# Causal masks added by TensorE in the bank of the row maxima, one plain maximum a head

## What is computed

```
# first block: 8 heads of 16, 4 key heads, window of 128 and 4 sink columns
allowed = (j <= i) & ((j < SINKS) | (j >= i - WINDOW + 1))
scores = jnp.where(allowed, q @ k.T * SCALE + directions, -jnp.inf)
# second block: 16 heads of 8, 4 key heads
scores = jnp.where(jnp.tril(ones(256, 256)), q @ k.T / np.sqrt(8), finfo.min)
# third block (second layer): 16 heads of 8, no mask
attn = jax.nn.softmax(scores, axis=-1); out = attn @ v
```

## Time and profile before

| | |
|---|---|
| three runs | 2305.39, 2350.81, 2354.41 us |
| median | 2350.81 us |
| span of the profiled execution | 2378.5 us |
| mean granted TensorE clock in it | 0.850 of full speed |
| PE, DVE, ACT, POOL busy | 91%, 48%, 38%, 17% |
| first pass | about 60 to 472 us |
| second pass | about 500 to 1240 us |
| expert network | about 1240 to 1560 us |
| third pass | about 1580 to 2180 us |

### The profile page before, as it was taken

One profiled execution on the slowest core, in us unless ns is written; L12 is line 12 of the kernel. 1 busy time (PEld: TensorE's weight loads), 2 busy tenths in 40 slices (PEclk: granted clock), 3 DMA queues, 4 the chain that ended last, 5 costly groups with the idle time before them and its releaser, 6 DMA issues.

```text
span 2378.5 us, 35332 instructions
## 1 busy us (share of the span) xinstructions
PE 2162.3 (91%) x11152; PEld 1350.9 (57%) x11152; DVE 1141.0 (48%) x4250; ACT 894.1 (38%) x1820; POOL 404.1 (17%) x643
## 2 busy tenths in 40 slices
PE   5999999879999999999989999969999999999490
PEld 3666666545555555555557888844555555554260
DVE  3344545354444444443428888845554545444102
ACT  1243434423343344343452222214554444554130
POOL 2111211121111121121100000022121212121505
PEclk8598989957686788786889999958998999999595
DMA  6000000000000000000000000010000000000132
GB/s 211 1 1 1 0 1 0 1 0 1 1 1 2 1 1 2 1 1 1 1 1 1 1 0 0 1 36 1 1 1 2 1 2 1 1 1 2 48 107 75
DMA packets 26218, 30.38 MB, mean 13 GB/s; under 512 B 3744, under 2 KB 19392, under 8 KB 25664
## 3 DMA queue, kind: packets, MB, share of 16 engines
q1 hardware_dynamic: 24000, 24.08, 3.2%
q0 software_dynamic: 2048, 4.20, 0.6%
HBM read 19.88 MB, written 8.39 MB: 12 GB/s over the span
## 4 chain that ended last, share of the span: by engine, by line
PE 86%; DVE 4%; issue 3%; POOL 2%; ACT 2%; another core or an unknown queue 1%; DMA 1%; SPq 0%; POOLq 0%; DVEq 0%; ACTq 0%
PE ps_out L1812 25%; PE ps_four L1794 8%; PE ps_four L997 5%; PE ps_max L1008 5%; PE ps_max L1764 4%; PE ps_max L1759 3%; PE ps_four L1718 3%; PE ps_four L1674 3%; PE ps_work L1699 3%; PE ps_max L1760 2%; PE ps_four L1699 2%; PE ps_work L1679 2%; PE ps_four L1787 2%; PE ps_four L1796 2%; PE ps_work L1658 2%
## 5 line engine op out<-in xcount | busy, mean ns | idle before, releaser
L1812 PE MATMUL ps_out<-attn_f,v_all 128*9 128x256 f32 (+3 forms) x2560 | 654.7, 384 | 5.8 <-ACT attn_f L1383 5.2
L1394 ACT ACTIVATE attn_f<-ps_four 128x384 f32<-128x384 f32 (+1 forms) x640 | 340.5, 532 | 627.2 <-PE ps_four L1796 618.4
L1812 PEld LDWEIGHTS ps_out<-attn_f,v_all 128*9 128x9 f32 (+1 forms) x2560 | 196.1, 96 | 273.9 <-issue 78.1
L1794 PE MATMUL ps_four<-q_st,k_st 26*128 26x256 f32 (+1 forms) x640 | 263.3, 411 | 0.2 <-DVE q_st L1602 0.2
L1581 DVE CUSTOM_DVE_ANT_0 ps_max<-ps_max,q_masks 128x128 f32<-128x128 f32 (+1 forms) x768 | 256.2, 377 | 0.0
L1588 DVE TENSOR_REDUCE row_max<-ps_max 128x2 f32<-128x512 f32 x256 | 170.1, 686 | 132.7 <-PE ps_max L1764 132.6
L1383 ACT COPY attn_f<-ps_out 9x512 f32<-9x512 f32 (+1 forms) x320 | 183.8, 575 | 132.1 <-PE ps_out L1812 132.1
L1794 PEld LDWEIGHTS ps_four<-q_st,k_st 26*128 26x128 f32 (+1 forms) x640 | 127.8, 200 | 75.6 <-issue 26.2
L1796 PE MATMUL ps_four<-q_st,k_st 26*128 26x256 f32 (+2 forms) x640 | 164.8, 258 | 0.0
L1574 DVE COPY wait_cell<-one 128x1 f32<-128x1 f32 x384 | 56.9, 148 | 186.3 <-PE ps_max L1760 181.2
L1008 PEld LDWEIGHTS ps_max<-wd,o_both 128*128 128x128 f32 x1024 | 134.7, 193 | 18.7 <-DVE o_both L904 8.3
(11 more groups left out here) (250 smaller groups left out, 3423.0 us busy)
## 6 DMA issues: line engine op xcount, KB each, us to landing
wd<-in_L_ffn_W SPq DMA_DIRECT2D x16, 256.0 KB, 2.6
gates_all<-in_select SPq DMA_DIRECT2D x3, 1024.0 KB, 7.3
x_all<-in_L_attn_x SPq DMA_DIRECT2D x8, 256.0 KB, 6.0
slots_dram<-attn_f SPq DMA_DIRECT2D x8, 256.0 KB, 5.5
h_tok<-slots_dram SPq DMA_DIRECT2D x8, 256.0 KB, 2.7
y_dram<-o_both SPq DMA_DIRECT2D x8, 256.0 KB, 2.4
out_x<-x_all SPq DMA_DIRECT2D x16, 128.0 KB
wgu<-in_L_ffn_Wg SPq DMA_DIRECT2D x1, 1024.0 KB, 5.8
```

What stands on the lines that cost most here:

```text
L1394: nc.scalar.activation(probs[:, h % 4, 0:w], ps_exp[:, h % 3, 0:w], ACT.Exp, scale=c.scale).then_inc(exp_done, 1)
L1794: nc.tensor.matmul(bank[:, 0:S], k_st[rows, r, g, 0:P], q_st[rows, r, g, :], start=not c.causal, stop=True, skip_group_check=True)
L1812: last = nc.tensor.matmul(ps_out[0:c.hd + 1, (h % 2) * S + first:(h % 2 + 1) * S], v_tok[c.index][:, r, kb, kv, :], probs[:, h % 4, kb * S ...
```

## The change

The row maxima get their masks as the exponentials do. TensorE first writes 384 columns of masks into the bank (ident_bf times three blocks), and the two score matmuls add onto them. VectorE takes one tensor_reduce over three blocks of 128 columns instead of two masked reductions, and no small copies. The second and the third block both belong to queries 128 to 255, so once a batch, after the last head, one small tensor_tensor takes the maximum of the two for all heads; the step "rows" waits for it by a new semaphore. The array masks now holds three blocks for each of the two orientations. exp_scores writes its masks by one matmul of 384 columns in both causal passes; in the second pass the middle block is zero, which VectorE sets at the start of that pass, and TensorE waits for that once.

```diff
-        masks = sb("masks", [P, 2, P], BF16)
+        masks = sb("masks", [P, 2, 3, P], BF16)
...
-        row_max = sb("row_max", [P, 2, BLK, 16])
-        wait_cell = sb("wait_cell", [P, 6])
-        q_masks = sb("q_masks", [P, 3, P])
+        row_max = sb("row_max", [P, 2, 3, 16])
...
-            nc.vector.tensor_copy(q_masks[:, 0, :], squares[:, 1, :])
-            nc.vector.tensor_copy(q_masks[:, 1, :], squares[:, 2, :])
-            nc.vector.tensor_copy(q_masks[:, 2, :], squares[:, 1, :]).then_inc(pro_dve, 1)
-            dve.wait_ge(pro_dve, 9)
...
-            nc.gpsimd.tensor_copy(masks[:], squares[:, 3:5, :])
+            for side, square in enumerate((1, 3)):
+                nc.gpsimd.tensor_copy(masks[:, side, 0:2, :], squares[:, square:square + 2, :])
+                nc.gpsimd.tensor_copy(masks[:, side, 2, :], squares[:, square, :])
...
                 dve.wait_ge(max_mm, hn + 1)
-                if c.causal:
-                    nc.vector.tensor_copy(wait_cell[:, h % 4:h % 4 + 1], one[:])
                 if h == 0:
                     at_least(dve, mt_mm, n - 1)
-                    if c.causal and not isinstance(n, int):
-                        nc.vector.tensor_copy(wait_cell[:, 4 + r2:5 + r2], one[:])
-                if c.causal:
-                    for k, (first, last) in enumerate(((0, P), (P, 3 * P))):
-                        ins = nc.vector.tensor_tensor_reduce(
-                            ps_max[:, h % 2, first:last], ps_max[:, h % 2, first:last],
-                            q_masks[:].rearrange("p n m -> p (n m)")[:, first:last], 1.0, LEAST, ALU.add, ALU.max,
-                            row_max[:, r2, k, h:h + 1])
-                    ins.then_inc(max_done, 1)
-                else:
-                    src = ps_max[:, h % 2, 0:c.q_cols()].rearrange("p (k s) -> p k s", k=BLK)
-                    nc.vector.tensor_reduce(row_max[:, r2, :, h], src, AX_X, ALU.max).then_inc(max_done, 1)
+                blocks = 3 if c.causal else 2
+                src = ps_max[:, h % 2, 0:c.q_cols()].rearrange("p (k s) -> p k s", k=blocks)
+                nc.vector.tensor_reduce(row_max[:, r2, 0:blocks, h], src, AX_X, ALU.max).then_inc(max_done, 1)
+                if c.causal and h == c.heads - 1:
+                    dve.wait_ge(max_done, hn + 1)
+                    nc.vector.tensor_tensor(row_max[:, r2, 1, 0:c.heads], row_max[:, r2, 1, 0:c.heads],
+                                            row_max[:, r2, 2, 0:c.heads], ALU.max).then_inc(row_max_done, 1)
...
-                    nc.vector.memset(q_masks[:, 1, :], 0.0).then_inc(window_open, 1)
-                    dve.wait_ge(window_open, 1)
+                    nc.vector.memset(masks[:, :, 1, :], 0.0).then_inc(window_open, 1)
...
                 if c.causal:
-                    nc.tensor.matmul(bank[:, 0:P], q_st[rows, r, g, 0:P], k_st[rows, r, g, 0:P], start=True, stop=True)
-                    nc.tensor.matmul(bank[:, P:3 * P], q_st[rows, r, g, P:S], k_st[rows, r, g, :], start=True,
-                                     stop=True).then_inc(max_mm, 1)
+                    nc.tensor.matmul(bank[:, 0:3 * P], ident_bf[:], masks[:, 0].rearrange("p n m -> p (n m)"),
+                                     start=True, stop=False, skip_group_check=True)
+                    nc.tensor.matmul(bank[:, 0:P], q_st[rows, r, g, 0:P], k_st[rows, r, g, 0:P], start=False,
+                                     stop=True, skip_group_check=True)
+                    nc.tensor.matmul(bank[:, P:3 * P], q_st[rows, r, g, P:S], k_st[rows, r, g, :], start=False,
+                                     stop=True, skip_group_check=True).then_inc(max_mm, 1)
...
                 if c.causal:
-                    nc.tensor.matmul(bank[:, 0:P], ident_bf[:], masks[:, 0, :], start=True, stop=False,
-                                     skip_group_check=True)
-                    nc.tensor.matmul(bank[:, S:S + P], ident_bf[:], masks[:, 0, :], start=False, stop=False,
-                                     skip_group_check=True)
-                    if c.window:
-                        nc.tensor.matmul(bank[:, P:S], ident_bf[:], masks[:, 1, :], start=False, stop=False,
-                                         skip_group_check=True)
+                    nc.tensor.matmul(bank[:, 0:3 * P], ident_bf[:], masks[:, 1].rearrange("p n m -> p (n m)"),
+                                     start=True, stop=False, skip_group_check=True)
...
-                    pe.wait_ge(max_done, HEADS_BEFORE[c.index] + (b + 1) * c.heads)
+                    if c.causal:
+                        pe.wait_ge(row_max_done, n + 1)
+                    else:
+                        pe.wait_ge(max_done, HEADS_BEFORE[c.index] + (b + 1) * c.heads)
...
+                if c.index > 0:
+                    pe.wait_ge(window_open, 1)
```

More of the change, by code:

```diff
@@ L22 @@
 LN_EPS = 1e-5
-LEAST = -3e38
 MASKED = -1e30
@@ L335, in adaln_two_layers @@
         max_done = sem("max_done")
+        row_max_done = sem("row_max_done")
         mt_mm = sem("mt_mm")
@@ L975, in pe_prologue @@
             last.then_inc(pro_pe, 1)
-            pe.wait_ge(pro_dve, 10)
+            pe.wait_ge(pro_dve, 9)
             pe.wait_ge(ones_ready, 2)
```

## The result

The changed kernel takes 2462.9 us (median of 4 runs, 2455.9 to 2483.7) against 2337.0 us of the kernel before (4 runs beside it, 2305.4 to 2354.4): 126 us more. The ratio that goes with the comparison, which leaves out runs over 1.5% above the fastest of their kernel, is 1.064 [1.054, 1.074]: slower.

The account below looks back on a forecast made before the run. The prediction took TensorE's instruction sequence to bound both causal passes. 40.4 us (first pass) plus 115.3 (second) plus 4 (openings) less 10 gave +150 us, 6.3%, or 2499 us on 2350.8; range 2430 to 2590 us.

Parts of the forecast that it names:

- Mask to strip: Causal heads' maxima: from the new 384-column mask matmul to the first score matmul, 0.26 us at the high clock.
- second head: Second head of a pair in the maxima, free before, now costs 0.68 us at the high level, 1.18 at the low.
- The credit for the step to a strip: Leading heads' masks: 0.09 us off where an all-partition matmul precedes, leaving 0.17 us; none behind L1812.
- Second pass, 115 us: Second causal pass's added time: 46.6 us leading heads, 49.8 second heads, 18.9 exponentials' masks; 115.3 us.
- the step that put 30% of the heads at the low level's prices: Second pass: 44% of its time at the low clock, weighted with the two matmul rates, made 30% of the heads.
- First pass, 40.4 us less a part of the 10: First causal pass's added time: 18.6 us leading heads, 22.4 second heads, -0.6 exponentials' masks; 40.4 us.
- 10 us back in all: PE's waits for row maxima, q_st and similar small ones: 10 us regained, bounds 0 and 30.
- Openings, 4 us: The 24 heads in the two openings, where PE partly waits for others: 4 us, between 0 and 11.
- DVE's busy time 160 us lower or more: Sign in the changed profile: VectorE's busy time falls at least 160 us, with PE no less late.
- Pairs still overlap: Rival: pairs' scores still overlap or masks hide neighbours' weight loads; 72 us fall away, +78 us, 2428 us; chance 0.04.
- the clock's rivals: Causal passes' clock: low longer, 2560 us (0.11); third pass's level, 2372 us (0.08); never low, 2285 us (0.05).
- the third one, given 0.05: Rival: the clock never falls in either causal pass; -66 us, 2285 us, faster; chance 0.05.

Follow-up runs that it names:

- e4: Changed kernel, but where a slot scores two heads both mask matmuls are issued first, then both heads' scores; median 2310.0 us.
- e2: Kernel before with only the exponentials' masks changed to one matmul of 384 columns; median 2390.1 us.
- e6: Kernel before with all mask matmuls of the change added, VectorE's masked reductions and small copies kept; median 2504.2 us.
- e1: Kernel before, unedited, run again for a second trace; 2323.3 us.
- e5: Changed kernel with no masks in the row maxima and the exponentials' masks as in the kernel before; for timing only; median 2329.4 us.
- e3: Changed kernel with the exponentials' masks as in the kernel before, so only the row maxima get the new masks; median 2454.9 us.
- e7: Changed kernel with four tiny copies a head added on VectorE; median 2438.9 us.
- e8: Changed kernel with only 128 of the 384 mask columns written ahead of the row maxima; for timing only; median 2365.3 us.
- e10: Changed kernel with masks first for all pairs except heads 4 and 5 of the second pass, right behind the combine; median 2336.7 us.
- e11: As e4, but in the second pass both kinds of masks write only blocks 0 and 2, leaving out the zero middle block; median 2310.3 us.
- e12: Kernel before with three 384-column mask matmuls added per second-pass batch, around the combine (heads 3, 4 and 5); median 2379.7 us.

## Why the prediction was right, and where it was not

**Direction and mechanism: right.** TensorE's sequence got longer and both causal passes are TensorE passes. The forecast was +6.3% and 2499 us; the medians differ by 5.4% (126 of 2337 us), and the ratio of the comparison says 6.4%. Own work is +127 us where the sum said +150, so the terms add up to some 20 us too much. That 6.3% meets 6.4% so closely is luck: the kernel's clock moves its time by more than the difference.

**Prices at the high level: right.** Mask to strip 0.27 (0.26 said), second head 0.69 (0.68), exponentials' mask +0.05 (+0.045). For a batch of the second pass at the high level they make 5.93 us (7 leading heads at 0.17, 5 at 0.26, 4 second heads at 0.68, 16 times 0.045); 6.15 was measured. The credit for the step to a strip is borne out: of e4's 4.07 us a batch, 0.80 are the exponentials' masks (e2) and four times 0.17 the second masks, which leaves 2.59 us for the twelve leading heads where these prices make 2.49; without the credit it would be 3.12. The Trainium skill (TensorE: Matmul & The Clock Gate, Part 1) states columns at 2.4 GHz plus 2.5 ns, by which 384 columns would take 0.163 us, an estimate. The traces agree where a mask follows a mask (0.172 us, e4) and not where a strip follows (0.26 us), which is where the change put every mask.

**Second pass, 115 us: mis-sized, own price about 92.** Two terms went wrong. The low-level prices were a little too high: 0.43 and 1.15 us for 0.46 and 1.18, and +0.11 for +0.14 on the exponentials. The larger error is the step that put 30% of the heads at the low level's prices. In the two profiles the second pass spends 321 us at the low level before and 318 after: there the low time did not grow with the work. A low stretch in the changed kernel is this window, with one at the high level beside it:

```profile
611.00:637.50 26.50, 26.50 (x148) 15.65 (x147) 9.56 (x27) 11.87 (x25) 4.30 (x8) 1.00 0.00 1
638.00:665.00 27.00, 27.00 (x76) 12.79 (x74) 6.90 (x17) 6.77 (x19) 3.75 (x6) 0.50 0.00 0
```

At equal low time an added matmul pushes other work out of the low stretch into the high level, and is paid at the high price wherever it stands: 15 x 6.15 = 92 us. Batches show it: one with 25 to 28 us of low clock took 48.7 us before, and one with 27 took 54.5 after, 5.8 more, no more than one without. With its own high-level prices throughout the prediction would have had 90 us here. That the low time as a whole stays the same is less certain. Mean clocks and medians of the table give, as 2 x (1 - clock) x time, 646 us of it in an execution before and 640 after, but 711 in e6, which has the same work on TensorE, and e1's second pass spent only 215 us there.

**First pass, 40.4 us less a part of the 10: mis-sized.** A batch took 1.42 us more where the prices say 2.4, 21 us in all. The difference is idle time of PE: in a batch at the high level it sums to 0.94 us before (0.35 of it at L1787 for q_st, 0.2 each at L1699 and L1724) and to 0.05 after. Of that 0.27 is VectorE's shorter work (e5), and the rest is waits that the new matmuls cover. The prediction had "10 us back in all"; the first pass alone gave some 15: between its first and last exponential PE stood idle for 18.1 us before and 3.1 after. Against e1, whose first pass took 385.5 us at 0.95, the changed one with 394.0 is 8.5 us longer, where 15 batches at +1.42 would be 21: the waits at the loop's start and the low stretches behind both are gone. This the prediction missed, for it looked for PE's waits in the sums of the earlier trace rows, read "4 times, longest 1.9", and did not ask why VectorE was late there. The answer stands in VectorE's own timeline, as idle time by "issue".

**Openings, 4 us: 7 measured** in the second pass's opening alone, 16 heads at the low level; what the first pass's opening cost can't be told from the scatter of its start, 56 to 61 us in the kernels with the maxima's matmuls of before. The sum is within the bounds. **VectorE's work: wrong, and without a price.** The sign "DVE's busy time 160 us lower or more" did not come: it is 64 lower. The reduction takes 0.56 us, not 0.52, and the sum of 256 and 108 us counted accumulator reads that run beside the next instruction. It did not matter, as PE hardly waits for VectorE. The rows step costs nothing, as said: PE waits for the small maximum only in the two openings, 0.95 us each, where before it waited 1.0 and 1.7 us for the masked reductions.

**The rivals.** "Pairs still overlap" is refuted in the timeline; e4 shows what it would have been worth, 53 us and not 72, since two masks still run one after the other. The clock stayed at 0.80 in the second pass of the profile and 0.870 over the runs, against 0.863: none of the clock's rivals came about for the kernel as a whole. In the first pass it did rise, to 0.98. And the third one, given 0.05, was near: the same instructions in e4's order have 0.98 in both causal passes. That the order of a few matmuls could carry the clock was nowhere in the argument.

## What to carry to other kernels

Read the distance from one matmul's start to the next one's by what follows it: here a full-height matmul between two that lie in different strips cost its own 0.26 us and the neighbours' overlap, 0.42 us more, and writing both masks first gave 0.52 us a pair back. Price added work at the level at which the displaced work ends up, not where the new instruction stands, if the low time in the traces does not grow with the work. Do not add up the busy times of instructions that may run beside each other; take the distance from one round of them to the next. Where runs of one kernel spread by 5% with the granted clock, compare at equal clock or by the period of one iteration at the high level: the periods of eleven kernels here add up to within 0.1 us (e2 and e3 give 6.12 us, the whole 6.15), while the medians hide it.

## What the runs showed of the hardware

- VectorE stops for 2.3 to 2.7 us at the start of loop iterations of the first pass, waiting for no engine, when its own loop body is long, and doesn't when it is shorter (e7 against after; q14 84 against 56 packets). A packet of the instruction queue starts 0.4 to 0.7 us into each of the twelve waits, which makes the loading of its instructions the reading by far the likeliest; how long a body may be was not measured.
- On VectorE the read of an accumulator runs beside the next reduction: both start at 709.33 in the lines above.
- In the second pass of before and after the clock falls 2 to 3.5 us behind the start of many combines, 16 matmuls of 36 columns (635.36 in the changed kernel), while PE is busy without a gap:

```profile
635.36 1.98 PE L1704 MATMUL ps_four<-strips,attn_f 128*128 128x36 f32 x16
...
637.80 1.42 PE L1796 MATMUL ps_out<-attn_f,v_all 128*9 128x256 f32 x4
639.14 0.50 PE L1745 MATMUL ps_max<-masks,ident_bf 128*128 128x384 bf16 x1
```

- How often it falls there goes with the matmuls elsewhere in the batch and their order: 10 of 14 in the changed kernel, 0 to 2 of 14 or 15 in e4, e8, e10 and e11. In e4 the order alone is changed, and its four runs have mean clocks of 0.893 to 0.928 where the changed kernel's four have 0.863 to 0.875. e12 speaks against full-height work next to the combine as what decides it, and e10 against the pair behind it alone. Nor is it a larger amount of masks (e8 has a third of the columns ahead of the maxima, and 1 of 14). What decides stays open; and as each count is from one execution, 5 of 14 and 8 of 14 are not to be told apart.
